# Second attention pass of a fused decoder kernel: the causal mask moved from TensorE products to GpSimd selections, with the parts in another order

## The reference

```python
qkv = (x @ Wqkv).reshape(b, t, 3, H, hd).transpose(2, 0, 3, 1, 4)
q, k, v = (qkv[0], qkv[1], qkv[2])
scores = jnp.einsum('bhqd,bhkd->bhqk', q, k) * hd ** (-0.5)
causal = jnp.tril(jnp.ones((t, t), bool))
scores = jnp.where(causal, scores, -jnp.inf)
attn = jax.nn.softmax(scores, axis=-1)
out = jnp.einsum('bhqk,bhkd->bhqd', attn, v)
```

## Time and profile before

| | |
|---|---|
| median of 3 runs | 242.68 us (242.04 to 242.95) |
| the profiled execution: its own time | 243.1 us |
| its span in the profile | 241.3 us |
| busy TensorE products / VectorE / ScalarE / GpSimd | 178.5 / 170.2 / 156.8 / 71.9 us |
| products L1754 and L1757, 128 of each, over the whole span | busy 17.3 and 18.4 us |

### The profile page before, as it was taken

How to read it: one execution, slowest core, us unless ns; L and a number is a source line. 1 busy time by engine, 2 the same in 40 slices (tenths; PEclk the granted TensorE clock), 3 DMA queues, 4 the chain that set the end, 5 groups by cost and what they waited for, 6 DMA issues and landing times.

```text
span 241.3 us, 4480 instructions
## 1 busy us (share of the span) xinstructions
PE 178.5 (74%) x1621; PEld 108.3 (45%) x1625; DVE 170.2 (71%) x495; ACT 156.8 (65%) x344; POOL 71.9 (30%) x113
## 2 busy tenths in 40 slices
PE   0223457698764787729956986899999999889894
PEld 0202423687521333205634533546655655544763
DVE  3758888959886988696794498678877977442511
ACT  4798995775983866993425563567865875886241
POOL 8031231014523044495018694101101110130210
PEclk9999999555799799998998898699999999999999
DMA  5999000000000000000002350413000000000011
GB/s 142 421 418 360 26 0 0 0 3 1 0 1 0 3 0 0 1 0 0 3 0 67 71 117 13 66 37 39 3 2 5 3 5 5 2 3 0 0 46 43
DMA packets 4635, 11.50 MB, mean 48 GB/s; under 512 B 1283, under 2 KB 2788, under 8 KB 3974
## 3 DMA queue, kind: packets, MB, share of 16 engines
q1 hardware_dynamic: 3654, 10.03, 12.4%
q0 software_dynamic: 960, 1.19, 2.1%
HBM read 8.23 MB, written 0.52 MB: 36 GB/s over the span
## 4 chain that ended last, share of the span: by engine, by line
DVE 33%; PE 27%; ACT 17%; POOL 13%; issue 6%; DMA 3%; SPq 1%; ACTq 0%; DVEq 0%; POOLq 0%
DVE negmax L1374 8%; PE ps L1771 6%; PE ps L1528 5%; POOL uh L460 4%; POOL KS L347 3%; ACT PT L804 2%; ACT fg L653 2%; PE ps L1710 2%; PE ps L1807 2%; ACT xhat L602 2%; DMA cw<-in_cond_w 2%; DVE mx L1265 2%; POOL rms L404 2%; ACT junk L510 2%; DVE u L1158 2%
## 5 line engine op out<-in xcount | busy, mean ns | idle before, releaser
L1374 DVE TENSOR_REDUCE negmax<-ps 128x1 f32<-128x384 f32 (+3 forms) x96 | 51.2, 593 | 13.7 <-PE ps L1712 13.5
L804 ACT ACTIVATE PT<-ps 128x1024 f32<-128x1024 f32 x40 | 39.5, 1031 | 20.3 <-PE ps L1757 20.2
L1710 PE MATMUL ps<-KS,QS 48*128 48x128 bf16 (+3 forms) x128 | 31.3, 314 | 1.5 <-DVE negmax L1374 0.6
L1539 PE MATMUL ps<-k_b 128*128 128x512 bf16 x100 | 25.7, 412 | 8.3 <-DVE prod L1312 4.4
L1751 PE MATMUL ps<-QS,KS 51*128 51x512 bf16 (+3 forms) x128 | 24.3, 311 | 1.7 <-DMA QS<-nmT 1.7
L1711 PE MATMUL ps<-k_b 64*128 64x128 bf16 x128 | 23.6, 224 | 0.0
L1712 PE MATMUL ps<-k_b 64*128 64x64 bf16 x128 | 21.3, 195 | 0.0
L1771 PE MATMUL ps<-PT,V 128*9 128x512 f32 (+3 forms) x256 | 20.4, 434 | 0.0
L404 POOL TENSOR_TENSOR rstd<-veps,mhalf 128x4 f32<-128x4 f32 x8 | 8.4, 1050 | 39.5 <-DVE veps L932 37.1
L1539 PEld LDWEIGHTS ps<-k_b 128*128 128x128 bf16 x100 | 10.1, 106 | 22.3 <-DVE prod L1312 4.9
L404 POOL TENSOR_TENSOR rms<-vms,mhalf 128x4 f32<-128x4 f32 x10 | 10.2, 1026 | 31.5 <-DVE vms L1132 31.5
(11 more groups left out here) (242 smaller groups left out, 459.2 us busy)
## 6 DMA issues: line engine op xcount, KB each, us to landing
w<-in_wa SPq DMA_DIRECT2D x2, 1152.0 KB, 9.6
lw<-in_l_w SPq DMA_DIRECT2D x1, 1280.0 KB
brow<-in_bcast_rows SPq DMA_DIRECT2D x1, 1152.0 KB, 15.4
mw<-in_main_w SPq DMA_DIRECT2D x1, 1024.0 KB, 12.4
KS<-part POOLq DMA_DIRECT2D x12, 64.0 KB, 3.4
QS<-part SPq DMA_DIRECT2D x12, 64.0 KB
cw<-in_cond_w SPq DMA_DIRECT2D x1, 576.0 KB, 4.5
xs<-in_x SPq DMA_DIRECT2D x1, 512.0 KB, 6.1
```

The source lines that it names most:

```text
L804: nc.scalar.activation(PT[n % 2][:, s, :], bank(2 * (use % 2), 2), ACT.Exp).then_inc(S["p_ready"], 1)
L1374: V.tensor_reduce(negmax[n % 2][:, qt, h0:h0 + nh], bank(S_BANKS[k % 3])[:, 0:nh * w].rearrange("p (h w) -> p h w", w=w), AX.X, ALU.max, n ...
L1539: T.matmul(bank(bk).rearrange("p (r n) -> p r n", n=P), ident_b, ident_b.unsqueeze(1).to_broadcast([P, NT, P]), start=True, stop=True)
L1710: T.matmul(dst, QS[b][rows, h, tok(qt)], KS[b][rows, h, 0:w], start=True, stop=False)
```

## The change

The second pass loses its two mask products in every block. Instead GpSimd sets the future entries of `PT` to zero after the exponential, with `affine_select` (`drop_future`): 7 selections per group, six of 128x256 elements and one of 128x512. ScalarE now signals `p_exp`, on which TensorE's next slot in the same banks waits; `values` waits for `p_ready`, which GpSimd now signals. The tables also change: in round n slots 1 and 2 of group n-2 stand behind items 0 and 1, slots 3 and 4 behind items 4 and 5, slot 0 of group n-1 behind item 9, and `values` is cut in three, behind items 8, 9 and 10. VectorE divides behind item 5 in place of item 3. ScalarE's order follows, the tail has two more slots of group 6, and GpSimd's inverse root and bias for batch 0 stand among the selections of the last group.

```diff
-E_OLD = {1: 3, 5: 4}
-E_NEW = {7: 0, 9: 1, 11: 2}
-PV_AT = {6: (0, 1, 3), 10: (2,)}
+E_OLD = {0: 1, 1: 2, 4: 3, 5: 4}
+E_NEW = {9: 0}
+PV_AT = {8: (0,), 9: (1, 3), 10: (2,)}
+DIVIDE_AT = 5
...
+            def drop_future(n, s):
+
+                diagonals = [(0, 2, L)] if s < 2 else [(0, 2, L), (3 * P, 2, L)] if s < 4 else [(0, 4, 2 * P)]
+                pool.wait_ge(S["p_exp"], 5 * n + s + 1)
+                for at, count, step in diagonals:
+                    v = PT[n % 2][:, s, :].rearrange("p (c w) -> p c w", w=step)[:, :, at:at + P]
+                    ins = nc.gpsimd.affine_select(v, v, [[0, count], [1, P]], ALU.is_ge, 0.0, base=0,
+                                                  channel_multiplier=-1)
+                ins.then_inc(S["p_ready"], 1)
...
+            for n in range(1, N_GROUPS + 1):
+                split_maxima(n - 1)
+                if n >= 2:
+                    for s in range(1, 5):
+                        drop_future(n - 2, s)
+                drop_future(n - 1, 0)
+            drop_future(N_GROUPS - 1, 1)
+            norm_root(0)
+            for s in range(2, 5):
+                drop_future(N_GROUPS - 1, s)
+            last_bias(0)
+            norm_root(1)
+            last_bias(1)
...
                 nc.scalar.activation(PT[n % 2][:, s, :], bank(2 * (use % 2), 2), ACT.Exp
-                                     ).then_inc(S["p_ready"], 1)
+                                     ).then_inc(S["p_exp"], 1)
...
-                    if i == 3 and n >= 3:
+                    if i == DIVIDE_AT and n >= 3:
                         divide(n - 3)
...
                 if use >= 2:
-                    pe.wait_ge(S["p_ready"], use - 1)
+                    pe.wait_ge(S["p_exp"], use - 1)
...
-                        T.matmul(dsts[half], KS[b][rows, h, tok(kt)], QS[b][rows, h, kt * P:L], start=True, stop=False)
-                    for half in range(2):
-                        r = half_rows(2 * half)
-                        T.matmul(dsts[half][:, 0:P // 2], k_of("pickLo", r), k_of("maskKlo", r), start=False, stop=False)
-                    for half in range(2):
-                        r = half_rows(2 * half)
-                        ins = T.matmul(dsts[half][:, 0:P], k_of("pickHi", r), k_of("maskKhi", r), start=False, stop=True)
+                        ins = T.matmul(dsts[half], KS[b][rows, h, tok(kt)], QS[b][rows, h, kt * P:L],
+                                       start=True, stop=True)
```

More of the change, by code:

```diff
@@ L67 @@
 KC, KC_N = _spans(("ident", P), ("count", 16), ("kone", 1), ("pickLo", P), ("pickHi", P), ("maskQlo", P),
-                  ("maskQhi", P // 2), ("maskKlo", P // 2), ("maskKhi", P))
+                  ("maskQhi", P // 2))
 W4_ROUND = (0, 1, 2, 3)
@@ L137 @@
     "minv_ready", "mod_copied", "mod_pe", "mod_ready", "mx_ready", "niT_pe", "ni_ready", "nm_copied", "nm_hi", "nm_left", "nm_mid", "nm_ready", "o_ready",
-    "p_ready", "par_ready", "part0", "part1", "part2", "pr_pe", "prod_ready", "pv_pe", "pv_ready", "qk_pe",
+    "p_exp", "p_ready", "par_ready", "part0", "part1", "part2", "pr_pe", "prod_ready", "pv_pe", "pv_ready", "qk_pe",
     "rest_ready", "picks_init", "picks_ready", "picked_pe", "picked_act", "picked_dve", "s_pe", "s_used", "sg_ready", "sig_ready", "silu_c", "st_pe", "stack_init", "stored", "ug_ready",
@@ L493, in split_maxima, with norm_root, last_bias @@
                                         ).then_inc(S["nm_ready"], 1)
-            for n in range(N_GROUPS):
-                split_maxima(n)
-            for b in range(B):
+            def drop_future(n, s):
[6 more added lines that the diff above has]
+                ins.then_inc(S["p_ready"], 1)
+            def norm_root(b):
                 pool.wait_ge(S["ln_var"], 3 * B + b + 1)
                 root(rstd[:, tiles(b)], veps[:, tiles(b)]).then_inc(S["ln_root"], 1)
+            def last_bias(b):
                 pool.wait_ge(S["xhat_ready"], B + b + 1)
@@ L823, in _ @@
                 if n >= 2:
-                    exp_slot(n - 2, 3)
+                    exp_slot(n - 2, 1)
+                    exp_slot(n - 2, 2)
                 copy_maxima(n - 1)
@@ L828, in _ @@
                 if n >= 2:
+                    exp_slot(n - 2, 3)
                     exp_slot(n - 2, 4)
                 exp_slot(n - 1, 0)
-                exp_slot(n - 1, 1)
                 if 2 <= n < N_GROUPS:
                     copy_values(n - 2)
-                exp_slot(n - 1, 2)
+            exp_slot(last, 1)
+            exp_slot(last, 2)
             copy_values(last - 1)
@@ L1835, in _ @@
             last = N_GROUPS - 1
-            exp_slot(last - 1, 3)
+            exp_slot(last - 1, 1)
+            exp_slot(last - 1, 2)
             bank_free(len(USES))
@@ L1840, in _ @@
             values_rows(last - 2)
+            exp_slot(last - 1, 3)
             exp_slot(last - 1, 4)
@@ L1913 @@
     mask_q = _np.where(i[None] > i[:, None], f32(BIG), f32(0))
-    mask_k = _np.where(i[:, None] > i[None], f32(BIG), f32(0))
     counts = _np.array([1.0 / WCOUNT[name] for name in WCOL] + [0.0] * (16 - len(WCOL)), f32)
@@ L1930 @@
         "consts": _np.concatenate([eye, _np.broadcast_to(counts, (P, 16)), (i % ROWS >= SROWS).astype(f32)[:, None],
-                                   eye[lo], eye[hi], mask_q[lo], mask_q[hi][:, P // 2:], mask_k[lo][:, :P // 2],
-                                   mask_k[hi]], 1),
+                                   eye[lo], eye[hi], mask_q[lo], mask_q[hi][:, P // 2:]], 1),
     }
```

## The result

The changed kernel takes 246.0 us (median of 4 runs, 245.31 to 246.39) against 242.63 for the kernel before on the same chip: ratio 1.0141, 95% interval 1.0115 to 1.0167. The forecast was 244.5, slower. The profiled execution took 246.0, its span is 244.3, 3.0 more than before.

What follows compares the result with a forecast made beforehand. It took a loop from split through turning, division, `values` and items 7 to 11 as the bound, not TensorE's total work. First rounds -1.0, steady rounds +2.85, GpSimd 0: +1.85 on the 242.68 median, 244.5 us, range 243.2 to 246.9.

Steps and rivals of the forecast that it cites:

- The loop: Steady round's chain of split, turning, division, `values` and last items: 9.0 us in place of 8.44, +0.57 in rounds 3 to 7.
- M: The moment when TensorE starts turning the maxima; times within a round are counted from it.
- an undelayed division: Division not held behind two more reductions: would help little, since item 8, ahead of `values`, needs item 5's bank.
- slot 4's two blocks (0.18): Mask products just ahead of `values`: the only 0.18 us of the 0.72 per round that lies on the loop.
- The rival in which TensorE's work sets the round: Steady rounds lose all 0.72 us of masks, to 7.72, if VectorE never starves; 237.2 us, chance 0.22.
- Round 1: Items 8 and 9 fill VectorE's wait for the maxima's DMA; split at 154.3 for 155.7, turning at 155.8 for 156.95: -1.15.
- Round 2: No division, but slot 0 waits for the maxima's DMA until M+3.85: 8.52 us in place of 8.37, +0.15.
- the clock stays low: Half of a rival with GpSimd as bound: TensorE stays at granted 0.50 for round 2, about +2; joint chance 0.11.
- The 0.50 at 151.5 to 155: TensorE's granted clock in the earlier trace, cited for the rival that it stays low in round 2.
- GpSimd and the tail: Selections of 0.58 and 1.06 us cost nothing in steady rounds or, at these middle values, in the tail.
- The comparison's row, 0.74: GpSimd's only profiled comparison, 2211 ns for 768 elements, used as upper estimate: 0.74 us for a 256-element selection.
- slow selections (+2.3): Tail's chain of selections at the upper end: finishes at 13.5 after M in place of 11.1, +2.3 us.

Runs made afterwards that it cites:

- e3: The changed kernel with the division behind item 3 again, nothing else; 244.59 us, ratio 1.0080.
- e5: The changed kernel with the division behind item 3 and the first piece of `values` behind item 6; 242.70 us, ratio 1.0000.
- e1: The kernel before with GpSimd's selections in place of the second pass's mask products, order of before kept; 242.05 us, ratio 0.9975.
- e2: The kernel before with its mask products and no selections, but the new tables and orders; 246.02 us, ratio 1.0153.
- e4: The changed kernel plus eight unread TensorE products in round 1, four ahead of turning the maxima, four behind item 9; 243.18 us, ratio 1.0040.
- e7: The kernel before plus the same eight unread products in round 1 as e4; 244.01 us, ratio 1.0056.
- e6: e1 plus the same eight unread products in round 1 as e4; 243.16 us, ratio 1.0036.
- e10: The changed kernel with each GpSimd selection preceded by an equal one on a spare tile; 246.77 us, ratio 1.0179.
- e12: The same kernel as e8, run once more for another profile; 240.67 us, ratio 0.9919.
- e8: e5 plus the eight unread products of e4 in round 1; 240.27 us, ratio 0.9878.
- e11: e6 with slots 0 to 2 of round 1 behind items 9, 10 and 11; 240.08 us, ratio 0.9881.

## Why the prediction was right, and where its size was off

**The loop: right, step by step.** Forecast and measured, from M: end of the division 2.88 and 2.88; `values` 3.02 and 3.02; item 9 4.00 and 4.00; `kt` 1 and 3 4.62 and 4.63; item 10 5.60 and 5.61; item 11 6.55 and 6.57; round 9.01 and 9.06. It is +0.62 for +0.57, over five rounds 0.25 more than forecast. That an undelayed division "would help little, since item 8 stands ahead of `values`" is shown by e3 (0.05 us), and e5 adds the other half: with the first piece behind item 6 the round is 8.44 again, 0.17 above e1's.

**The masks on the loop: right.** I put slot 4's two blocks (0.18) on the loop and nothing else of the 0.72 us. e1 gives 0.17, the pair after and e2 0.15. The rival in which TensorE's work sets the round wanted 7.72 and no kernel came near it: the lowest steady round was 8.26.

**Round 1: right in kind.** The forecast was -1.15, measured -1.36. The split started 6.41 us behind M (153.56 less 147.15) where I had 6.33; the turning followed 1.21 later, not 1.5, because what I had queued ahead of it cost nothing.

**Round 2: the term that was mis-sized.** I had "8.52" and "+0.15", at the full clock. It measured 10.72, +2.35. With the clock held, e4 has 8.53: the walk was right, and its premise, that round 2 runs at the full clock as before, was wrong. (Its start for kt 1 and 3, "M+4.13", is 0.03 below the sum of its own terms, 3.85, 0.22 and 0.09.) I had listed "the clock stays low" as a rival with about +2 and a part of 0.11; it came on top of the forecast and is 2.2 us of it. The 0.50 at 151.5 to 155 was there to see the earlier trace rows, and so was the work that the change takes from TensorE there. That the two are tied is shown by three pairs of one order with and without the masks (before and e1, e2 and after, e7 and e6) and by e4; which part of the removed work matters stays open.

**GpSimd and the tail: no cost, right; the sizes too high.** A selection took 0.41 us (forecast 0.58, ends 0.22 and 0.94), the wide one 0.64 (1.06). In the steady round slot 3's selections end at M+3.46 (187.06) and `kt` 1 and 3 start at M+4.63: 1.2 us of room, more than the 0.82 that e10 adds. The 0.43 us that I had worked out by the Trainium skill (GPSIMD Engine Reference, Performance pitfalls for Q7 kernels) for a body that compares and selects is the nearest of all the numbers I had for 256 elements. The agreement is chance: by the same rate the selection of 512 elements would be an estimate of 0.87, and it took 0.64. The comparison's row, 0.74, was too high. (The second exponential's 6.1 behind the last M comes out as 6.2, which changes nothing in the tail's sum.)

**Not foreseen: the first M.** It is 0.82 us earlier than in the profile before, in a part that the change doesn't touch. In the profiles of e1 to e12 it lies between 146.27 and 147.44; the 147.97 of before is the latest of all. In the first layer the mean granted clock was 0.50 from 42.7 to 63.2 us before and 0.67 in the same stretch after. e8 and e12 are one kernel, and their first M lies at 146.58 and 147.44: two executions of the same program differ there by as much. So I take it for chance; what sets it stays open.

**The sum.** 1.85 forecast, less 0.82 (first M), less 0.21 (round 1), plus 2.20 (round 2), plus 0.25 (loop), less 0.3 (tail) is 2.97, the span's 3.0. By medians it is 3.4, as the profiled execution of before was 0.5 above its median.

**What was luck.** The time lies inside the range of 243.2 to 246.9, but not for the range's reason. Its upper end stood for slow selections (+2.3), which cost nothing; the clock's 2.2 us, which I had kept apart as a rival, took that room, and an early first M gave 0.82 back. The range doesn't follow from its terms either: a round 0.15 either way gives 0.75 over five rounds, so 243.8 below, and 247.6 above with the selections' 2.3. The direction doesn't hang on the clock: e4, with the clock held, is still slower than before (ratio 1.0040, 1.0021 to 1.0059).

## What to carry to other kernels

In an order written by hand, ask of each long piece what stands behind it and which engine runs dry meanwhile: one piece behind item 8 in place of 6 cost 0.6 us per round with no instruction added. Cutting a piece and spreading it isn't better in itself: each part now had a critical item behind it. Where a short stretch of a profile shows a granted clock of 0.50, give the change's effect there at both levels before trusting the sum, and put filling work only where TensorE waits anyway: the same four products behind item 9 stood in e4, where the time fell, and cost 1.82 us on the chain in e7. Look at more than one execution, since the clock falls in some and not in others (e8 and e12). The fastest kernels here (e11 at 240.08, 1.2% below before; e8 and e12, one kernel, 1.2% and 0.8% below) keep the selections, and have the first piece behind item 6 and a first round of their own.

## What the runs showed of the hardware

- Rounds 1 and 2 took 18.33 us at mean granted clocks of 0.53 and 0.69 (after) and 15.66 at 1.00 (e4), with eight products more. In the same order and with the same idle products, removing the mask products left the clock at 0.50 for 13.6 us in place of 6.9, and round 2 took 10.60 in place of 8.52 (e6 and e7).
- One kernel in two executions (e8 and e12) had a clock of 0.50 from 145.1 to 162.1 in one and of 1.00 through the same rounds in the other.
- TensorE was busy 5.26 of 6.80 us ahead of the fall at 147.7 in the changed kernel, and 6.05 of 6.80 ahead of the same place in e4, where it didn't fall:

```profile
140.90:147.70 6.80, 5.26 (x52) 2.86 (x52) 6.45 (x12) 1.90 (x4) 5.77 (x11) 1.00 0.36 65
```
```profile
140.60:147.40 6.80, 6.05 (x54) 3.02 (x54) 6.52 (x13) 1.77 (x3) 5.80 (x11) 1.00 0.36 67
```

- `affine_select` in float32 on GpSimd, in place: 409 ns for 128x256 and 637 for 128x512, so by these two widths an estimate of 0.89 ns per element and a start of some 0.18 us; back to back, in e10, 406 and 634.
